# Two value tiles of the 32-wide attentions projected inside the heads, and every projection inside the heads written through the context's bank

## The reference, cut to what matters

```python
def attention(q, k, v, mask):
    scores = jnp.einsum('bhqd,bhkd->bhqk', q, k) / jnp.sqrt(jnp.float32(HD))
    scores = scores * mask - 10000.0 * (1.0 - mask)
    probs = jax.nn.softmax(scores, axis=-1)
    return jnp.einsum('bhqk,bhkd->bhqd', probs, v)
...
q, k, v = jnp.split(ln_out @ w_qkv + b_qkv, 3, axis=-1)
...
attn_out = ctx @ w_ao + b_ao
x = hidden_states + attn_out
```

## Time and profile before

| | |
|---|---|
| median of 3 runs | 4241.41 us |
| profiled execution, its time | 4250.26 us |
| its span in the profile | 4248.5 us |
| TensorE (matmuls) busy | 3740.6 us, 88% |
| VectorE busy | 2618.1 us, 62% |
| ScalarE busy | 2156.9 us, 51% |
| GpSimd busy | 1669.7 us, 39% |
| mean granted TensorE clock | 0.948 |

### The profile page before, as it was taken

The page is one execution under the profiler, slowest core; times in us unless marked ns, Lnnn a source line. Parts: engine busy times, 40 slices in busy tenths (PEclk is TensorE's granted clock), DMA queues, the critical chain, the costliest instruction groups (busy, mean ns, idle before and its releaser), DMA issues. The chain is left out here.

```text
span 4248.5 us, 66434 instructions
## 1 busy us (share of the span) xinstructions
PE 3740.6 (88%) x24448; PEld 2278.7 (54%) x24448; DVE 2618.1 (62%) x5675; ACT 2156.9 (51%) x4272; POOL 1669.7 (39%) x1865
## 2 busy tenths in 40 slices
PE   7988899898888989989888998998988889899898
PEld 4544565545545456555554545655555454565555
DVE  5765646666576564566657656456665765646665
ACT  5655733434666573343366657334336675733433
POOL 4554542232454454223245444422324544542222
PEclk9999999899999999999989999999999999999899
DMA  4032211102204222010220322101022032220102
GB/s 135 15 107 64 81 69 41 59 21 100 75 15 122 55 83 71 32 59 31 90 76 26 108 65 75 69 31 59 31 90 77 27 108 65 75 69 31 59 32 98
DMA packets 94558, 276.11 MB, mean 65 GB/s; under 512 B 25472, under 2 KB 25984, under 8 KB 73088
## 3 DMA queue, kind: packets, MB, share of 16 engines
q1 hardware_dynamic: 94208, 271.58, 19.8%
HBM read 201.24 MB, written 4.19 MB: 48 GB/s over the span
## 5 line engine op out<-in xcount | busy, mean ns | idle before, releaser
L805 POOL TENSOR_SCALAR probs<-probs,row_inv 128x512 f32<-128x512 f32 x1024 | 693.1, 693 | 643.9 <-DVE row_inv L720 643.9
L664 ACT ACTIVATE probs<-probs,row_max 128x512 f32<-128x512 f32 x1024 | 733.1, 725 | 130.8 <-DVE row_max L736 129.6
L559 PE MATMUL ps<-ident,probs 128*128 128x128 f32 x4096 | 609.8, 291 | 170.6 <-ACT pT L658 144.3
L559 PEld LDWEIGHTS ps<-ident,probs 128*128 128x128 f32 x4096 | 481.2, 147 | 381.1 <-ACT pT L658 206.9
L658 ACT ACTIVATE pT<-ps 128x512 f32<-128x512 f32 x768 | 429.8, 602 | 113.2 <-PE ps L559 112.7
L369 PE MATMUL ps<-mix,wring 128*128 128x512 f32 x1024 | 471.0, 596 | 3.5 <-DMA wring<-in_blocks_dram 3.4
L534 PE MATMUL ps<-kstack,qstack 96*128 96x512 f32 (+1 forms) x1024 | 383.4, 469 | 16.7 <-DMA qstack<-hi 7.1
L736 DVE CUSTOM_DVE_ANT_0 probs<-ps,maskA 128x512 f32<-128x512 f32 x512 | 329.3, 681 | 43.9 <-PE ps L534 43.9
L736 DVE CUSTOM_DVE_ANT_0 probs<-ps,neg 128x512 f32<-128x512 f32 x512 | 340.5, 685 | 8.9
L369 PEld LDWEIGHTS ps<-mix,wring 128*128 128x128 f32 x1024 | 191.2, 190 | 198.7 <-issue 179.3
L1532 POOL TENSOR_TENSOR hinv<-hvar,minus_half 128x32 f32<-128x32 f32 x24 | 146.2, 6092 | 377.3 <-DVE hvar L1254 377.3
(11 more groups left out here) (177 smaller groups left out, 7056.4 us busy)
## 6 DMA issues: line engine op xcount, KB each, us to landing
wring<-in_blocks_dram SPq DMA_DIRECT2D x151, 1024.0 KB, 5.0
qstack<-hi SPq DMA_DIRECT2D x256, 64.0 KB, 2.0
kstack<-hi SPq DMA_DIRECT2D x256, 64.0 KB, 2.0
maskA<-in_mask_dram SPq DMA_DIRECT2D x9, 1024.0 KB, 7.4
rows<-in_rows_dram SPq DMA_DIRECT2D x8, 1024.0 KB, 4.6
qstack<-hi SPq DMA_DIRECT2D x256, 32.0 KB, 2.0
qstack<-lo SPq DMA_DIRECT2D x128, 64.0 KB, 2.0
kstack<-lo SPq DMA_DIRECT2D x128, 64.0 KB, 2.0
```

Source lines behind the costliest of these rows:

```text
L559: ins = nc.tensor.transpose(tile[:, qc * P:(qc + 1) * P], probs[:, m % PSLOTS, qc, kc * P:(kc + 1) * P], ident[:, :])
L664: nc.scalar.activation(p, p, ACT.Exp, bias=row_max[:, n % PSLOTS, qc:qc + 1], scale=-1.0, accum_out=row_sum[:, n % PSLOTS, qc:qc + 1]).the ...
L805: nc.gpsimd.tensor_scalar(p, p, row_inv[:, (n - 1) % PSLOTS, qc:qc + 1], 1.0, ALU.mult, ALU.mult)\
```

## The change

The projections inside the heads are now named by a table: q2 in head 0, k2 in head 1, value tile 2 in head 2, value tile 3 in head 3, q3 in head 4, k3 in head 5. So q and k stay where they were, and value tiles 2 and 3 move from before the heads into heads 2 and 3, in both attentions. All six now write bank 7 instead of a bank of the ring. They share it one after the other: each waits, before its first matmul, until ScalarE (q, k) or VectorE (values) has taken out the one before (`BEFORE`), and the first context product waits until k3 has been taken out. VectorE adds the bias of value tiles 2 and 3 at the end of its work on heads 2 and 3. GpSimd's order does not change, nor does attention 0.

```diff
+                self.projects = {0: ('q', 2), 1: ('k', 2), 2: ('v', 2), 3: ('v', 3), 4: ('q', 3), 5: ('k', 3)}
+                if self.shared:
+                    self.projects = {}
...
+        BEFORE = {('q', 2): None, ('k', 2): ('q', 2), ('v', 2): ('k', 2), ('v', 3): ('v', 2), ('q', 3): ('v', 3), ('k', 3): ('q', 3)}
...
+        def in_heads(A, kind, g):
+            return not A.shared and g >= 2
...
+        def project_bank(A, kind, g):
+            return OBANK if in_heads(A, kind, g) else ring.bank(*((kind, A.tag) if kind == 'k' and A.shared else (kind, A.tag, g)))
...
+        def project_tile(pe, A, kind, g):
+
+            if not in_heads(A, kind, g):
+                return take(pe, *((kind, A.tag) if kind == 'k' and A.shared else (kind, A.tag, g)))
+            if BEFORE[kind, g] is not None:
+                before, b = BEFORE[kind, g]
+                pe.wait_ge(*(dve_emptied if before == 'v' else act_emptied).when(before, A.tag, b))
+            return ps[:, OBANK, :]
...
-            tile = take(pe, 'q', A.tag, g) if tile is None else tile
+            tile = project_tile(pe, A, 'q', g) if tile is None else tile
...
-        def pe_values(pe, A, tiles=range(C)):
-            w_wait(pe, A.vblk)
-            for tc in tiles:
-                to_N(pe, take(pe, 'v', A.tag, tc), weights(A.vblk), A.src, tc, n=A.vcols, base_=A.voff,
-                     fin=tile_ready.reach('v', A.tag, tc))
+        def pe_v(pe, A, tc, fcs=range(C), tile=None):
+            if tc == 0 and 0 in fcs:
+                w_wait(pe, A.vblk)
+            tile = project_tile(pe, A, 'v', tc) if tile is None else tile
+            to_N(pe, tile, weights(A.vblk), A.src, tc, n=A.vcols, base_=A.voff, fcs=fcs,
+                 fin=tile_ready.reach('v', A.tag, tc) if C - 1 in fcs else None)
+            return tile
...
                 pe_k(pe, A, 0)
                 pe_queries(pe, A, (1,))
                 pe_k(pe, A, 1)
-                pe_values(pe, A)
+                pe_v(pe, A, 0)
+                pe_v(pe, A, 1)
             if t == 2:
                 pe_queries(pe, A)
-                pe_values(pe, A, (2, 3))
...
                         if m >= 0 and mi == 0 and vg >= 0:
 
                             if kc == 0:
+                                if vg == 0 and not A.shared:
+                                    pe.wait_ge(*act_emptied.when('k', t, 3))
                                 if first and vg > 0:
...
-                    if not A.shared and g + 2 < A.groups and i < 2:
-                        part = (pe_q, pe_k)[i](pe, A, g + 2, fcs=(2 * half, 2 * half + 1), tile=None if half == 0 else part)
+                    if n in A.projects:
+                        kind, c = A.projects[n]
+                        part = {'q': pe_q, 'k': pe_k, 'v': pe_v}[kind](pe, A, c, fcs=(2 * half, 2 * half + 1),
+                                                                       tile=None if half == 0 else part)
...
-            nc.scalar.activation(split[:, s, :], ps[:, ring.bank(*label), :], ACT.Identity, bias=bias,
+            nc.scalar.activation(split[:, s, :], ps[:, project_bank(A, kind, g), :], ACT.Identity, bias=bias,
...
-                for step in (('x0', 'e0', 'x1', 'e2', 'x2', 'x3') if A.shared else ('e0', 'e1', 'x0', 'x1', 'e2', 'e3', 'x2', 'x3', 's')):
-                    if step == 's' and not A.shared and g + 2 < A.groups and i < 2:
-                        act_split(act, A, 'qk'[i], g + 2)
+                for step in (('x0', 'e0', 'x1', 'e2', 'x2', 'x3', 's') if A.shared else ('e0', 'e1', 'x0', 'x1', 'e2', 'e3', 'x2', 'x3', 's')):
+                    if step == 's' and A.projects.get(n, 'v')[0] != 'v':
+                        act_split(act, A, *A.projects[n])
...
         def dve_attention(dve, A):
             t = A.tag
             if t < 2:
-                dve_values(dve, A, range(C))
+                dve_values(dve, A, range(C) if A.shared else range(2))
...
                         inverse(n - 1, 1)
                     if n < A.heads:
                         add_max(n, 2 * half + 1)
+                if A.projects.get(n, 'q')[0] == 'v':
+                    dve_values(dve, A, (A.projects[n][1],))
...
                 g, i = divmod(n - 1, 4)
-                if not A.shared and g + 2 < A.groups:
-                    if i == 1:
-                        pool_split(pool, A, 'q', g + 2)
-                    if i == 2:
-                        pool_split(pool, A, 'k', g + 2)
+                if A.projects.get(n - 2, 'v')[0] != 'v':
+                    pool_split(pool, A, *A.projects[n - 2])
...
                     dve_norm(dve, 'ln2', xn, lambda tc: residual(dve, 1, tc))
-                    dve_values(dve, A2, range(C))
+                    dve_values(dve, A2, range(2))
                     dve_attention(dve, A2)
```

More of the change, by code:

```diff
@@ L372, in to_T, with to_N @@
                 m.then_inc(*fin)
-        def to_N(pe, tile, w, src, tc, n=H, base_=0, fin=None, ready=None):
-            for fc in range(C):
+        def to_N(pe, tile, w, src, tc, n=H, base_=0, fin=None, ready=None, fcs=range(C)):
+            for fc in fcs:
                 if ready is not None:
@@ L379, in to_N @@
                 m = nc.tensor.matmul(tile[:, 0:n], src[:, fc, tc * P:(tc + 1) * P],
-                                     w[:, fc * H + base_:fc * H + base_ + n], start=(fc == 0), stop=(fc == C - 1))
-            m.then_inc(*fin)
+                                     w[:, fc * H + base_:fc * H + base_ + n], start=(fc == 0), stop=(fc == C - 1),
+                                     skip_group_check=(len(fcs) < C))
+            if C - 1 in fcs:
+                m.then_inc(*fin)
         def dve_stats(dve, tag, tc):
@@ L477, in pe_k @@
             label = ('k', A.tag) if A.shared else ('k', A.tag, g)
-            tile = take(pe, *label) if tile is None else tile
+            tile = project_tile(pe, A, 'k', g) if tile is None else tile
             to_T(pe, tile, weights(A.kblk), A.src, 0 if A.shared else g, base_=A.koff, fcs=fcs, ready=ready,
@@ L503, in pe_attention @@
                 pe_queries(pe, A, (0,))
-                pe_values(pe, A)
+                for tc in range(C):
+                    pe_v(pe, A, tc)
                 pe_queries(pe, A, (1, 2, 3))
@@ L688, in dve_values @@
             t = A.tag
-            if t < 2:
+            if t < 2 and 0 in tiles:
                 dve.wait_ge(sems['rows_in'], 16 * (t + 1))
@@ L692, in dve_values @@
                 dve.wait_ge(*tile_ready.when('v', t, tc))
-                tile = ps[:, ring.bank('v', t, tc), :]
+                tile = ps[:, project_bank(A, 'v', tc), :]
                 if A.shared:
@@ L1595, in _ @@
                     pe_k(pe, A2, 1)
-                    pe_values(pe, A2, (0, 1))
+                    pe_v(pe, A2, 0)
+                    pe_v(pe, A2, 1)
                     pe_norm_turn(pe, 'ln2', xn)
```

## The result

The changed kernel takes 4286.61 us (median of 5 runs, 4285.37 to 4289.39) against 4241.41 (4233.95 to 4247.2): a ratio of 1.0113, 95% interval 1.0097 to 1.0129. It is slower by 45 us (1.1%), and the forecast was 4285. The profiled execution has a span of 4283.6 us against 4248.5.

The account below looks back on a forecast made before the run. VectorE was taken to bound heads 7 to 15, a chain of waits through TensorE heads 0 to 6. Per sample -2.65 + 4.7 + 4.7, with the clock 10.95; four samples 44 us, median 4285, range 4256 to 4304.

Parts of the forecast that it names:

- What bounds the heads: VectorE sets the pace in heads 7 to 15, 5.10 us a head; that rest gives back none of the loss.
- The hand-overs: Bank 7 passed between projections in heads 1 to 6: about 4.0 of the 4.7 us lost per attention.
- the next half's scores stand behind it, and VectorE behind those: In the heads, TensorE cannot go round a waiting projection, so scores and VectorE's mask multiplies wait too.
- the walk: Timeline of heads 0 to 8: splits end 4.09 us after the second mask multiply; head 8 at 50.2 against 45.46.
- The copies: Before the heads, copies to `qstack` end the wait: attention 1 starts 2.65 us sooner, attention 2 gains nothing.
- The clock: Half clock after TensorE's rests before the heads: 1.5 us in attention 1, 1.7 in attention 2.
- head 1: Half clock may return after TensorE's 2.2 us hand-over wait there: between 0 and 1.7, taken as 0.5 us an attention.
- The sum: Both attentions: 6.75 us a sample, 10.95 with the clock; 44 for four samples, 4294 profiled, 4285 as median.
- The ring is relieved: Rival for the heads: bank 7 ends transposes' wait for a split; 7.7 us a sample gained, 4211; chance 0.03.
- The clock costs nothing: Rival: after TensorE's rests the clock stays, or falls only where VectorE has work in hand; 4268; chance 0.22.
- Dearer: Rival: every rest brings the long slow stretch and hand-overs cost 5.7; 16 us a sample, 4306; chance 0.07.
- The hand-overs are hidden: Rival: in the heads TensorE reaches each projection late enough; 4236, or some 4250 with the clock; chance 0.13.

Follow-up runs that it names:

- kernel 1: Changed kernel with k2 and k3 back in the ring, value tiles 2 and 3 still in heads 2 and 3: 4246.38 us, ratio 0.9995.
- kernel 4: Changed kernel with ScalarE's split put ahead of its head's last two exponentials, all projections still sharing bank 7: 4247.13 us, ratio 0.9999.
- kernel 5: Changed kernel plus 12 small idle matmuls (48 instructions) at the start of each sample: 4238.27 us, ratio 0.9997 to the kernel before.
- kernel 8: Changed kernel with k2 and k3 in the ring, plus 12 small idle matmuls at each sample's start: 4203.09 us, ratio 0.9916.
- kernel 2: Changed kernel with all four value tiles before the heads again; q2, k2, q3, k3 still through bank 7: 4269.11 us, ratio 1.0055.
- kernel 3: Changed kernel with idle matmuls filling TensorE's rests before the heads (3 in attention 1, 9 in attention 2): 4234.98 us, ratio 0.9976.
- kernel 10: Kernel before with only attention 1's value tile 3 moved, into head 2; bank 7 for it, q2, q3; k2, k3 in the ring: 4219.84 us.
- kernel 11: Kernel 10 plus 12 small idle matmuls at the start of each sample: 4175.61 us, ratio 0.9856 to the kernel before.
- kernel 9: Changed kernel with k2 and k3 in the ring and both rests before the heads filled with idle matmuls (3 and 9): 4185.13 us, ratio 0.9881.

## Why the prediction was right

**What bounds the heads.** Right. VectorE's pace in heads 7 to 15 is unchanged (head 8's distance to the last multiply is 38.2 us in both kernels, but for one sample of the kernel before, 39.4), and nothing lost before is given back.

**The hand-overs.** The step on which the forecast rested, "the next half's scores stand behind it, and VectorE behind those", holds; kernels 1 and 4 take the wait away in two ways and each returns about 40 us. The splits end where the walk put them, 4.1 us behind their head's second mask multiply (3456.52 to 3460.62). The size was a little low: a lap is 6.64 us instead of 6.45, since a projection from rest costs 0.26 more than one in a stream and not 0.1. From 0b to head 8 the changed kernel has 48.2 us where it was 43.0, 5.2 more instead of 4.7. (The 0.04 us from a score tile to its multiply stands in no row; the chain above has 0.03, from 3463.13 to 3463.16. Nothing hangs on it.)

**The copies.** Too small. I counted the landing from the end of the 24th issue; the chain shows its 1.99 us directly behind the third of the last four issues, that is from the start of the last. The gain at attention 1's start is 3.1 to 3.6 us, not 2.65. The rows come behind a stall of the sync engine's copies, so where it is absent (kernels 5 and 8) the gain is 4.3 us. In attention 2 nothing was gained, as forecast: TensorE waited 8.48 us for the same copies.

**The clock.** Right at the starts: 1.2 to 1.3 us in attention 1 (forecast 1.5), 1.0 to 1.7 in attention 2 (1.7), and 0.5 more before attention 2's first multiply (its first two score tiles take 1.22 us instead of 0.75). Wrong for head 1: forecast 0.5 an attention, measured none here, behind a rest of 1.9 to 2.0 us. Behind a rest of 2.40 to 2.44 us at the same place (kernel 2, kernel 3, attention 1 of kernel 5), 20 attentions in all, it is 1.7 us in eight, 0.8 to 1.0 in four and nothing in eight. Before attention 2 of kernel 10, rests of 1.9 and 2.0 us were followed by it in two samples, and rests of 1.6 us in the other two were not. What decides in between is not shown. So the clock's cost at the start could not simply be taken off: in attention 1 of kernel 3 it came back at the hand-over, in attention 2 mostly not. The Trainium skill's rule ("TensorE: Matmul & The Clock Gate", Part 1: 1.2 GHz after idling, 2.4 after sustained work) agrees with the rows at both starts (0.52 and 0.51 behind the rests).

**The sum.** By start times it is 9.9 us a sample (39.6 for four) against a forecast of 10.95: a larger gain (-0.6) and no clock in head 1 (-1.0) against dearer hand-overs (+1.0) make up most of it. That the median came within 2 us has luck in it. The sum gave 4294 for the like of the profiled execution, and that of the changed kernel took 4285.4, 9 us less; the median agrees because the 8.9 us taken off for it had no counterpart, the changed kernel's profiled execution being the fastest of its runs. The kernels here also move by over 30 us with the places of TensorE's instructions, and of this the prediction has nothing.

**The rivals.** "The ring is relieved" is half true. Kernels 10 and 11 show the relief at 1.3 to 1.5 us an attention; in the change it is buried under the hand-overs. "The clock costs nothing" falls with the late 0b of the changed kernel and with kernel 9. "Dearer" had hand-overs at 5.7 and the clock at every rest: they cost 5.2, and the clock did not fall at head 1. "The hand-overs are hidden" was priced at 4236 to 4250; kernel 1, which makes it true, took 4246.

## What to carry to other kernels

One buffer passed down a chain of producers costs little only if what empties it stands early enough in its own engine's stream: look up where the release stands, not how long it takes, and what is queued behind the wait. Move only as much work as the next thing that is late allows (here one tile of four, in one of two attentions), because what is moved beyond it mostly buys a rest, and the rests before the heads of the changed kernel were all followed by half clock. When an edit adds or drops instructions, compare against a kernel shifted by as many idle ones before putting the difference down to the edit.

## What the runs showed of the hardware that was not expected

Bursts of 128 small matmuls (32 rows by 128 columns) in the recurrent layers stand still for 1.4 to 2.2 us at fixed places of TensorE's stream, 12 to 15 times a launch (22 to 26 us), with nothing released at their end. Shifting the stream by 48 instructions removed every one of them in all seven kernels in which it was tried, and made the kernel before faster by 34 to 39 us, more than most edits to the work itself.

The traces show what stands beside each gap. Every page has this queue:

```profile
q8 instruction: 202, 3.31, 0.3%
```

Its 202 packets are of 16 KB. A burst without a gap takes 1.9 us (2.1 to 2.4 in seven that such a packet starts just ahead of). In all 80 gaps of over 1 us (kernel before, changed, 1, 2, 4, 10) such a packet starts 0.6 to 1.5 us after the burst's first matmul, and the burst goes on 1.2 to 1.6 us after the packet has landed. In the bursts without a gap, those of the shifted kernels among them, a packet inside starts 1.3 us or more after the first matmul. So TensorE most likely runs out of instructions while the next block is loaded, and the shift moves the load to the burst's end or out of it. This is argued from times that coincide in every case; no run moved the loads alone, so it is not shown as a cause. How far a shift has to be was not tried.

Beside this, kernels 8 and 9 differ by 11 us outside the two attentions, and that stays open.
